# Expert passes with routing rows spread out of a DRAM scratch; GpSimd scales the activated gate, VectorE forms the low part

## The reference, cut to what matters

```python
# layer 0: 16 experts of width 64, 4 chosen, and a shared expert
scores = jax.nn.sigmoid(xf @ gate_w.T)
# ... the best 2 of 4 groups, and in them the best 4 experts, into comb (T, 16)
h = jax.nn.silu(h1) * h3
y = jnp.einsum('tei,edi,te->td', h, w2, comb)
z = jax.nn.silu(xf @ ws1.T) * (xf @ ws3.T) @ ws2.T
# layer 1: 8 experts of width 256, the best 2, weights from a softmax over the two
```

## Time and profile before

| | us |
|---|---|
| median of 3 runs | 2029.44 (2028.14 to 2033.78) |
| the profiled execution, its own time | 2030.13 |
| its span, first to last instruction | 2028.2 |
| PE busy | 1744.3 (86%) |
| DVE busy | 1439.9 (71%) |
| ACT busy | 960.2 (47%) |
| POOL busy | 729.4 (36%) |
| mean granted clock of TensorE | 0.944 of full |

### The profile page before, as it was taken

How to read it: one execution, slowest core, us unless ns; L and a number is a source line. 1 busy time by engine, 2 the same in 40 slices (tenths; PEclk the granted TensorE clock), 3 DMA queues, 4 the chain that set the end, 5 groups by cost and what they waited for, 6 DMA issues and landing times. The chain is left out here.

```text
span 2028.2 us, 28208 instructions
## 1 busy us (share of the span) xinstructions
PE 1744.3 (86%) x8712; PEld 1247.0 (61%) x8712; DVE 1439.9 (71%) x4268; ACT 960.2 (47%) x1557; POOL 729.4 (36%) x659
## 2 busy tenths in 40 slices
PE   3898959899899899977998799999967775999998
PEld 2666735555555555535766577777856564777776
DVE  5878748777777777827788567777667765677675
ACT  2444414565565555654444355555532221555554
POOL 3444421312312312124445455555521001555555
PEclk9999968999999999987999899999978887999999
DMA  3000011111111111010000100000000000000000
GB/s 103 1 1 0 1 29 22 26 22 27 21 22 30 18 22 28 12 39 37 0 1 0 40 1 1 1 0 0 1 0 0 0 1 1 1 11 6 5 11 11
DMA packets 18248, 28.08 MB, mean 14 GB/s; under 512 B 2753, under 2 KB 10178, under 8 KB 18130
## 3 DMA queue, kind: packets, MB, share of 16 engines
q1 hardware_dynamic: 15874, 23.68, 5.4%
q10 hardware_dynamic: 2256, 2.96, 0.5%
HBM read 10.83 MB, written 2.10 MB: 6 GB/s over the span
## 5 line engine op out<-in xcount | busy, mean ns | idle before, releaser
L976 ACT ACTIVATE att_probs<-banks 128x1024 f32<-128x1024 f32 (+3 forms) x384 | 305.9, 811 | 197.1 <-PE banks L887 195.3
L1101 DVE CUSTOM_DVE_ANT_0 banks<-banks,att_mask 128x128 f32<-128x128 f32 (+3 forms) x512 | 234.3, 525 | 73.5 <-PE banks L868 73.0
L868 PE MATMUL banks<-arena 128*128 128x512 f32 (+3 forms) x768 | 250.1, 407 | 27.5 <-DMA arena<-att_parts 15.1
L1016 POOL TENSOR_SCALAR_AFFINE_SELECT att_probs<-att_probs 128x512 f32<-128x512 f32 x128 | 81.2, 635 | 422.7 <-ACT att_probs L976 422.7
L868 PEld LDWEIGHTS banks<-arena 128*128 128x128 f32 x768 | 133.1, 198 | 151.6 <-issue 91.9
L461 POOL TENSOR_TENSOR ffn1b_hid_l<-ffn1b_hid,ffn1b_hid_h 128x512 fp32r<-128x512 f32 x128 | 165.0, 1292 | 130.0 <-ACT ffn1b_hid_h L415 130.0
L461 POOL TENSOR_TENSOR ffn1a_hid_l<-ffn1a_hid,ffn1a_hid_h 128x512 fp32r<-128x512 f32 x128 | 165.3, 1293 | 125.2 <-ACT ffn1a_hid_h L415 125.2
L887 PE MATMUL banks<-arena 128*128 128x512 f32 (+3 forms) x768 | 205.2, 352 | 0.5 <-ACT att_probs L976 0.4
L1103 DVE TENSOR_REDUCE att_mx<-banks 128x1 f32<-128x512 f32 x256 | 162.2, 684 | 32.0 <-PE banks L868 31.8
L906 PE MATMUL banks<-att_probs,att_v_aug 128*32 128x512 f32 (+3 forms) x1536 | 167.7, 509 | 0.6 <-POOL att_probs L1016 0.5
L887 PEld LDWEIGHTS banks<-arena 128*128 128x128 f32 x768 | 137.7, 191 | 26.4 <-ACT att_probs L976 11.3
(11 more groups left out here) (404 smaller groups left out, 4176.3 us busy)
## 6 DMA issues: line engine op xcount, KB each, us to landing
arena<-att_parts SPq DMA_DIRECT2D x16, 384.0 KB
arena<-att_parts SPq DMA_DIRECT2D x128, 48.0 KB
w_raw<-in_ffn_w_dram SPq DMA_DIRECT2D x6, 352.0 KB, 5.5
out_dram<-x SPq DMA_DIRECT2D x8, 256.0 KB, 2.3
setup_raw<-in_ffn_w_dram SPq DMA_DIRECT2D x3, 576.0 KB, 6.4
w_raw<-in_ffn_w_dram SPq DMA_DIRECT2D x3, 320.0 KB, 6.2
setup_raw_sel<-in_consts_dram ACTq DMA_DIRECT2D x1, 576.0 KB, 10.9
x<-in_L_attn_x_dram ACTq DMA_DIRECT2D x1, 512.0 KB, 8.0
```

What stands on the lines that cost most here:

```text
L868: mm = pe.matmul(bank[:, at:at + width], q_st[:, n % 3, t * P:(t + 1) * P], k_pad[:, n % 2, j, c * G:c * G + width], start=True, stop=True ...
L976: act.activation(probs[:, unit % NPROB, 2 * pair:2 * pair + 2, 0:c], score_ps[:, pair, :, 0:c], ACT.Exp, scale=SCALE).then_inc(exped, 1)
L1101: ins = dve.tensor_tensor_reduce(now, now, mask[:, G - width:G], 1.0, -3e38, ALU.add, ALU.max, best)
```

## The change

- The L319 matmuls, `sel` and the routing banks go. `combt` (now plain float32, one row per expert) is written by SP to a scratch `weight_rows` in DRAM, and SP reads each expert's row back with the same row for 64 (layer 0) or 128 (layer 1) partitions, into `share`, 8 slots of 128 x 512 in SBUF: one write and 16 or 8 reads a group.
- `scale` moves to POOL and multiplies `sil` by `share`. The ninth chunk of layer 0, the shared expert, isn't scaled.
- `low` moves to DVE, and stands behind `hide` of the following chunk.
- Gate and up have three banks each, and `sil`, `scl`, `hid`, `hid_h`, `hid_l` three buffers. PE still projects two chunks behind (`LAG = 2`).
- The normalisation moves to ACT (scale and shift), with a second small POOL step for the shift; statistics are formed two groups ahead; `slot` has other places.
- All groups are written out, without a hardware loop. Weights for the next stage come in pieces of up to 512 columns through three buffers, two per group, in SP's queue behind the routing reads.
- Setup loses the transfer and cast of `sel`; unused constants go. Attention and the gated stage keep their instructions, except for the source of one 1 x 1 copy.

```diff
-                if c % PER == 0:
-                    e = c // PER
-                    if c == 0:
-                        pe.wait_ge(comb_t, g + 1)
-                    mm = pe.matmul(comb_ps[:, comb_bank(q, c), :], sel[:, e * P:(e + 1) * P], combt[:, q, :],
-                                   start=True, stop=True)
...
+            for g in range(g0, end):
+                sp.wait_ge(comb_t, g + 1)
+                sp.dma_start(k.rows[g % 2, 0:NE, :], combt[:, g % 2, :]).then_inc(rows_out[g % 2], 16)
+                sp.wait_ge(rows_out[g % 2], 16 * (g // 2 + 1))
+                for e in range(SLOTS):
+                    if g > g0:
+                        sp.wait_ge(scaled, (g - 1) * NSCALED + (e + 1) * PER)
+                    for h in range(HALVES):
+                        n, at = e * HALVES + h, h * P // HALVES
+                        sp.dma_start(share[at:at + P // HALVES, e, :],
+                                     k.rows[g % 2, n, :].partition_broadcast(P // HALVES)).then_inc(share_in[e], 16)
...
+    LAG = 2
+    NB, NH = 3, 3
...
+        slot = dict(stats=7, aggr=7, rstd=8, norm=8, turn=0, xh=0, xl=0, logit=2, lout=2, lturn=3,
+                    r1=3, r2=4, r3=5, r4=5, cturn=6, yout=2, yturn=4, y=4)
...
+            for h in range(g0 - 2, end):
                 for c in range(NC):
+                    if h >= g0:
+                        up_and_gate(h, c)
+                        if c >= LAG:
+                            project(h, c - LAG)
+                        elif h > g0:
+                            project(h - 1, NC - LAG + c)
...
+            def scale(g, c):
                 num = g * NC + c
-                pool.wait_ge(high_cut, num + 1)
-                pool.tensor_tensor(hid_l[:, n, :], hid[:, n, :], hid_h[:, n, :].bitcast(F32), ALU.subtract)\
+                pool.wait_ge(silu_done, num + 1)
+                at_least(pool, hidden, num - NB + 1)
+                if c % PER == 0:
+                    pool.wait_ge(share_in[c // PER], (g + 1) * HALVES * 16)
+                pool.tensor_tensor(scl[:, num % NB, :], sil[:, num % NB, :], share[:, c // PER, :], ALU.mult)\
+                    .then_inc(scaled, 1)
...
+            def low(num):
+                dve.wait_ge(high_cut, num + 1)
+                dve.tensor_tensor(hid_l[:, num % NH, :], hid[:, num % NH, :], hid_h[:, num % NH, :].bitcast(F32),
+                                  ALU.subtract).then_inc(low_cut, 1)
...
+            for h in range(g0 - 2, end):
+                for c in range(NC):
+                    if h >= g0:
+                        if slot["y"] == c and h > g0:
+                            add(h - 1)
+                        hide(h, c)
+                        if h * NC + c > g0 * NC:
+                            low(h * NC + c - 1)
```

More of the change, by code:

```diff
@@ L403, in silu @@
+            def silu(g, c):
                 num = g * NC + c
                 act.wait_ge(gate_done, num + 1)
-                if not (isinstance(num, int) and num < 2):
-                    act.wait_ge(scaled, num - 1)
-                act.activation(sil[:, n, :], gate_ps[:, n, :], ACT.Silu).then_inc(silu_done, 1)
-            def high(g, q, c):
-                n = (q * NC + c) % 2
-                num = g * NC + c
+                at_least(act, hidden, num - NB + 1)
+                act.activation(sil[:, num % NB, :], gate_ps[:, num % NB, :], ACT.Silu).then_inc(silu_done, 1)
@@ L464, in body @@
-            def body(g, q, more):
-                start = isinstance(g, int) and g == g0
-                for c in range(NC):
-                    if c > 0:
-                        low(g, q, c - 1)
-                    elif not start:
-                        low(g - 1, 1 - q, NC - 1)
-                    if place(g, c) is not None:
-                        ahead.low(pool, place(g, c))
-                    if more and slot["rstd"] == c:
-                        invert(g + 1)
+                pool.wait_ge(silu_done, num + 1)
@@ L484, in _ @@
-            body(g0 + NG - 2, 0, True)
-            body(g0 + NG - 1, 1, False)
-            low(g0 + NG - 1, 1, NC - 1)
+            for h in range(g0 - 2, end):
+                for c in range(NC):
+                    if h >= g0:
+                        if c < NSCALED:
+                            scale(h, c)
+                        if piece_at(h, c) is not None:
+                            ahead.low(pool, piece_at(h, c))
+                    chain(h, c, (("rstd", invert),))
         @block.vector
@@ L605, in scale @@
                 dve.wait_ge(up_done, num + 1)
-                dve.tensor_tensor(scl[:, n, :], sil[:, n, :], comb_ps[:, comb_bank(q, c), :], ALU.mult).then_inc(scaled, 1)
-            def hide(g, q, c):
-                n = (q * NC + c) % 2
-                num = g * NC + c
-                dve.wait_ge(scaled, num + 1)
-                if not (isinstance(num, int) and num < 2):
-                    dve.wait_ge(low_cut, num - 1)
-                dve.tensor_tensor(hid[:, n, :], scl[:, n, :], up_ps[:, n, :], ALU.mult).then_inc(hidden, 1)
@@ L616, in body @@
-            def body(g, q, more):
-                real = not (isinstance(g, int) and g < g0)
-                for c in range(NC):
-                    if real and slot["y"] == c and not (isinstance(g, int) and g == g0):
-                        add(g - 1)
-                    if real:
-                        scale(g, q, c)
-                        hide(g, q, c)
-                    if more:
-                        for s, f in (("stats", stats), ("aggr", aggr), ("norm", norm), ("xl", xl), ("r1", r1),
-                                     ("r2", r2), ("r3", r3), ("r4", r4)):
-                            if slot[s] == c:
-                                f(g + 1, 1 - q)
+                dve.tensor_tensor(hid[:, num % NH, :], (scl if c < NSCALED else sil)[:, num % NB, :],
+                                  up_ps[:, num % NB, :], ALU.mult).then_inc(hidden, 1)
@@ L648, in parcel @@
+            low(end * NC - 1)
+            add(end - 1)
 def parcel(arena):
@@ L1572, in weights @@
         def weights(layer, get):
[L1573 removed]
+            NC = C0 if layer == 0 else C1
             def ws(name, n):
```

461 lines of the change are left out of this document (201 added, 260 removed).

## The result

The changed kernel takes 2208.97 us, median of 6 runs (2203.18 to 2221.02). The kernel before, on the same chip, takes 2029.08 (2028.12 to 2033.78). The ratio is 1.0887, 95% interval 1.0861 to 1.0913: slower by 180 us. 2160 was forecast, in a range that holds 2209. The profiled execution took 2221.0 us, the longest of the six, with a span of 2219.3 and a mean granted clock of 0.928; before, the span was 2028.2 and the clock 0.944. The spans differ by 191 us, the medians by 180.

A forecast was written before the change was run, and what follows sets the result against it. TensorE bounded layer 1, with waits in layer 0. 2030.1 + 102 (layer 1) + 8 - 1 (layer 0) - 1 (setup) - 2 (ends) + 16 (starts) + 6 (weight pieces) + 5 (clock) = 2163, written 2160; range 2065 to 2238.

The forecast's parts named there:

- The loop: Expert passes: gate matmuls through Silu, scl, hid, low part to gate(c+2), 5.18 us for two chunks; 2.68 a chunk taken.
- full exclusion cycle of 2.77: GpSimd and VectorE: if each also waits for the other, scl, hid and low part run serially, 2.77 us a chunk.
- The two engines: VectorE's low part and GpSimd's scl exclude each other; VectorE waits as second, whether GpSimd does no row showed.
- Extras of a layer-1 group: Statistics, output addition, routing steps and TensorE's transposes and router between chunks: 2.5 us a group, bounds 1 and 4.
- Layer 0: Its two expert passes: 28.0 us a group against 27.0 and 28.1, so +8 us in ffn0a, -1 in ffn0b.
- Starts: Start of each expert pass: exposed DRAM write and read plus a second small GpSimd step, +4 us a pass, +16.
- The DRAM trip: Routing rows written and read back: hidden inside a pass, exposed at its start, write 2.4 and read 2.5 us.
- rival 4: Routing rows land late at group boundaries, some 1.5 us in each of 28: about 2200 us; chance 5%.
- The clock: TensorE's granted clock: new waits seldom long enough to lower it; 0 to +60 us, +5 taken.
- rival 3: Waits let the clock fall often, one to two half-clock chunks per group on full exclusion: about 2240 us; chance 13%.
- Rival 2: The loop forms but the engines' long products do not exclude each other, 2.59 us a chunk: about 2080; chance 20%.
- Rival 1: TensorE stays the bound, 63 us of routing matmuls saved, +16 for starts: about 1985 us; chance 9%.

The follow-up runs named there:

- low_psum: Changed kernel with the low part's second input read from the up product's PSUM bank (low part not computed, for time alone): 2141.26 us.
- early_stats: Changed kernel with the statistics and reciprocal root two slots earlier in layer 1, one in layer 0, normalisation left in place: 2134.51 us.
- low_first: Changed kernel with VectorE forming the low part of chunk c-1 before the hid product of chunk c instead of behind it: 2078.19 us.
- the version with the order mended: Changed kernel with scl on VectorE ahead of hid, low part on GpSimd, statistics earlier, down matmuls three chunks behind: 1949.24 us, ratio 0.9584.

## Why the prediction was right

The direction, the order of size and the loop as the main mechanism were right. The sum was 49 us short of the median, and 58 short of the profiled execution, in which the terms below are measured. Two terms were too small, the extras of a group and the clock; two were too large, the loop and the starts, and it was luck that they made up for part of it.

**The loop: right.** The walk gave 2.59 us a chunk without and 2.77 with full exclusion; I took 2.68. Measured in the group without preparation: 2.55, and 2.52 without exclusion (low_psum). The walk was 0.07 too long, so the term was 2 us a group too high. The full exclusion cycle of 2.77 did not form: in the last group of ffn1b only one of the 15 scl products that start in it lasted much over its own time (1654 ns, the others at most 1342), because the low part was mostly over before Silu had made scl ready.

**The two engines: right in kind.** VectorE as the second waits for GpSimd, as the earlier trace rows had shown for small steps, and now the long one as well: low parts of up to 1.75, comb with a median of 1.27 for 0.19. That GpSimd is stretched as the second, which no row before could show, is now shown: up to 1.74 for 1.29. The Trainium skill (SBUF — State Buffer, "Who interferes with whom") says that the second to issue blocks fully, whichever it is. The trace agrees in both directions to within 0.15 us: the scl at 1991.24 is 0.40 over its own time where 0.55 of the low part were left to run, and the low part at 1997.33 is 0.58 over where 0.71 of scl were left. By the cycle of 2.77 the sum is not about 15 us more, as the prediction has it: 0.09 us in each of 256 layer-1 and 128 scaled layer-0 chunks is 35. It would have come nearer to the time, but by a cycle that did not form.

**Extras of a layer-1 group: the mis-sized term.** Taken 2.5 us, bounds 1 and 4. Measured: 50.4 - 16 x 2.55 = 9.6 us. Even with the steady term 2 us lower, a group has 50.4 where the forecast had 45.4, and the two passes grew by 77 + 81 = 158 where 102 was forecast. The hid starts of one group of ffn1b show where it lies. They are apart by 4.1 and 4.1 (transposes, high and low cut of the next group's x), 5.6 (router), 3.7 (hs, df and the output addition), 3.9 (choice of experts), 3.4 (comb, blocked) and 5.0 (normalisation), the rest by 1.7 to 3.0. The step of the sum that failed is "short steps hide; what exceeds it counts", with TensorE's steps counted by half. I had reckoned each by its own duration on its own engine. In a loop without slack it is its duration plus the wait in front of it that counts, wherever in the loop it stands. The router in the timeline of the changed kernel:

```profile
1980.23 0.56 PE L298 MATMUL banks<-ffn1b_xh,arena 128*128 128x512 f32 x1
...
1981.01 0.63 PE L300 MATMUL banks<-ffn1b_xh,arena 128*128 128x512 f32 x1
1981.68 0.60 ACT L382 ACTIVATE ffn1b_logits<-banks 128x512 f32<-128x512 f32 x1 [3.32 <-PE banks L300]
1982.96 0.60 ACT L402 ACTIVATE ffn1b_sil<-banks 128x512 f32<-128x512 f32 x1 [0.68 <-PE banks L319]
...
1983.63 1.30 POOL L443 TENSOR_TENSOR ffn1b_scl<-ffn1b_sil,ffn1b_share 128x512 f32<-128x512 f32 x1 [4.82 <-ACT ffn1b_sil L402]
```

Three matmuls and an eviction of their result into SBUF, 2.05 us from 1980.23 to 1982.28, delay Silu, scl and hid in turn. Before, the same steps cost less because there was slack; but even there the trace would have warned: groups of 39.5 us against 16 x 2.23 = 35.7 make 3.8 us of extras, so the upper bound of 4 was hardly more than what the kernel before already paid. And the normalisation on ACT, called a gain off the path, costs a wait of 2.47 us in front of Silu; early_stats got 74 us from ending it, with all that followed from it.

**Layer 0: too low.** With 28.0 us a group, 8 and -1 us were forecast for the two passes, and 6 for the weight pieces; the passes grew by 17.3 and 10.0. The same preparation steps come once in nine chunks there; which of them costs what was not taken apart.

**Starts: near.** +4 a pass forecast, +3.4 measured in ffn1b, and 7.5 in place of 15 for all four with the setup. The other three stretches before a pass grew by 1.8, 0.5 and 1.7; why by less was not taken apart. The second small GpSimd step, L435, took 0.20 us where 1.0 was put.

**The DRAM trip: hidden, as said.** The share's read takes 3.0 and 4.5 us where 2.5 was taken by the row of a store; it stayed hidden inside the passes, and rival 4 did not happen.

**The clock: too low.** +5 us were put for it. A mean over the kernel hides what it did, since attention is in it; the layer-1 passes show it. These windows run from first to last hid of ffn1b, before and after:

```profile
1708.90:2018.80 309.90, 300.89 (x1333) 239.94 (x1331) 220.60 (x521) 160.41 (x289) 169.65 (x134) 0.99 0.02 7
```

```profile
1820.60:2211.40 390.80, 323.26 (x1257) 234.10 (x1257) 210.43 (x474) 170.40 (x312) 179.35 (x139) 0.94 0.14 46
```

And these stand around the router step above, after:

```profile
1977.60:1979.40 1.80, 0.00 (x0) 0.00 (x0) 1.80 (x3) 0.63 (x1) 1.22 (x1) 1.00 0.00 0
1980.40:1983.60 3.20, 3.20 (x9) 2.46 (x9) 0.16 (x1) 1.24 (x3) 0.00 (x0) 0.50 0.00 0
```

TensorE stands idle for 1.8 us, waiting for a low part, and soon after works at a granted clock of 0.50, the 1.2 GHz level. The router's matmuls and the next chunk's gate and up matmuls then start about 0.42 us apart (0.36 to 0.43) in place of 0.233. In groups two to seven of ffn1b such a stretch falls on the router step and another on the first chunks of the group, so two of the three longest places above, 4.1 and 5.6, are partly clock. Over the same groups of early_stats, which has the same loop, the router's distance is 4.5 us three times and 3.3 twice at a clock of 1.00, and 5.2 once at 0.67; the changed kernel has 5.6 to 6.1 there, at 0.70 to 0.72.

Counted in the trace after, 96 of the 128x512 matmuls of ffn1b and 83 of ffn1a start 0.40 to 0.45 us behind the one before them; before the change there were 6 and none. What they take over 0.233 adds up to 35 us in the two passes, 1 us before. As an estimate, that is the most that these matmuls can account for of the 158 us, because some of it would have been waited anyway. So rival 3's mechanism did happen, at a smaller size, although its own sign, a clock below 0.9 in the layer-1 passes, did not show (0.93 and 0.92). It comes from the waits and does not replace them: in the last group the clock is 1.00 and a chunk still takes 2.55 us, and low_first keeps a mean clock of 0.930, inside the 0.926 to 0.935 of the changed kernel, and is 131 us faster. The gains of early_stats and low_psum came with a clock that fell less often: in their layer-1 passes 57 and 65 matmuls are that slow, where the changed kernel has 179. No run separates the clock's share.

**The rivals and the signs.** Rival 4 came nearest to the time (2200) and rival 3 next (2240), the first with a wrong cause, the second with one that is a part of it. Rival 2 fell with the stretched products; and low_psum, which has the loop without the exclusion as rival 2 has it, took 2141 and not 2080: its extras are 46.0 - 16 x 2.52 = 5.7 us a group where rival 2 put 1.5. Rival 1 was wrong for this order, and near for the version with the order mended. Of the signs, TensorE at 80% and its wait for the low part in most chunks came as said. The steady distance of 2.55 was the sign for the loop without exclusion, not for the cycle.

## What to carry to other kernels

Before a product is moved to another engine, walk the loop from an engine's matmul back to itself, count the chunks that it spans, and divide; a step of chunk c-1 that is issued behind one of chunk c costs a whole lag. Read what the kernel already pays for its steps between chunks by comparing a group that has them with one that has none; without slack each of them costs its duration and its wait. Here, moving work off the bound engine paid only after the order, the lag and the due times of the preparation had been set again for it. Read the granted clock in the window of the stage and of its longest chunks, not as a mean over the kernel.
